# GpSimd waits for each indirect store, and for each tile's gathers, before it issues the next

## The reference

```python
x = layernorm(x + attention(x))            # 16 heads of 16, causal
x = layernorm(x + shared(x) + routed(x))
# routed: sigmoid scores over 16 experts, top 2 of (score + bias), the two scores scaled to sum 1;
# routed = sum over a token's two experts e of
#          weight_e * (silu(x @ gate_e) * (x @ up_e)) @ down_e      256 -> 2 x 128 -> 256
```

## Time and profile before

| | |
|---|---|
| Timed runs | 985.47, 985.3, 978.0 us |
| Span of the profiled execution | 975.7 us |
| Between its span and the median of the runs | 9.6 us |
| PE, DVE, ACT, POOL busy | 88%, 68%, 49%, 31% |
| Mean granted TensorE clock | 0.943 |
| Section 0's stores on GpSimd, first start to last start | 691.54 to 732.16 us |
| Pairs on PE | 737.83 to about 910 us |
| Section 1's gathers, first start to last start | 917.02 to 960.67 us |

### The profile page before, as it was taken

The page is one execution under the profiler, slowest core; times in us unless marked ns, Lnnn a source line. Parts: engine busy times, 40 slices in busy tenths (PEclk is TensorE's granted clock), DMA queues, the critical chain, the costliest instruction groups (busy, mean ns, idle before and its releaser), DMA issues. The chain is left out here.

```text
span 975.7 us, 18404 instructions
## 1 busy us (share of the span) xinstructions
PE 854.0 (88%) x5476; PEld 478.9 (49%) x5477; DVE 660.1 (68%) x1527; ACT 476.2 (49%) x686; POOL 300.0 (31%) x368
## 2 busy tenths in 40 slices
PE   7979799999999989999999997799898999999300
PEld 4635434444444434444444432687556777777200
DVE  6428688888888887888888870489892122466364
ACT  3423266656666656656666566455322444444100
POOL 3423312211112111221112211442477500464373
PEclk9979899999999999999999999889899999999755
DMA  8773855444764266425754000710126745766443
GB/s 285 193 205 131 162 67 75 100 97 59 131 85 89 36 117 118 68 38 106 130 66 57 9 2 25 235 65 23 60 103 210 232 137 152 207 207 211 157 126 95
DMA packets 82464, 113.95 MB, mean 117 GB/s; under 512 B 8945, under 2 KB 60401, under 8 KB 82417
## 3 DMA queue, kind: packets, MB, share of 16 engines
q1 hardware_dynamic: 57808, 78.01, 38.1%
q0 software_dynamic: 6720, 18.88, 5.9%
q10 hardware_dynamic: 17888, 16.41, 5.2%
HBM read 62.55 MB, written 50.33 MB: 116 GB/s over the span
## 5 line engine op out<-in xcount | busy, mean ns | idle before, releaser
L658 ACT ACTIVATE work<-ps 128x1024 f32<-128x1024 f32 (+3 forms) x384 | 293.8, 811 | 185.5 <-PE ps L725 185.3
L335 DVE TENSOR_REDUCE m_neg<-ps 128x1 f32<-128x512 f32 (+3 forms) x432 | 265.6, 662 | 29.2 <-PE ps L320 18.7
L629 POOL TENSOR_SCALAR_AFFINE_SELECT work<-work 128x512 f32<-128x512 f32 x128 | 81.2, 634 | 394.4 <-ACT work L658 390.0
L317 PE MATMUL ps<-stacks 96*128 96x512 bf16 (+3 forms) x528 | 151.9, 332 | 1.5 <-DVE m_neg L335 1.5
L725 PE MATMUL ps<-stacks 99*128 99x512 bf16 (+3 forms) x528 | 124.6, 329 | 6.4 <-PEq L371 4.8
L335 DVE TENSOR_REDUCE m_neg_late<-ps 128x1 f32<-128x384 f32 (+3 forms) x176 | 106.7, 636 | 27.4 <-PE ps L320 27.4
L740 PE MATMUL ps<-work,vg 128*32 128x512 f32 (+3 forms) x1056 | 112.5, 498 | 1.6 <-POOL work L629 1.6
L320 PE MATMUL ps<-mask_b,ident_b 128*128 128x128 bf16 x512 | 100.3, 223 | 0.0
L317 PEld LDWEIGHTS ps<-stacks 96*128 96x128 bf16 x528 | 50.0, 98 | 95.0 <-DVE m_neg L335 48.8
L1243 DVE TENSOR_TENSOR work<-work,ps 128x256 f32<-128x256 f32 x48 | 20.2, 421 | 106.7 <-ACT work L1062 106.7
L1421 PE MATMUL ps<-wgu,work 128*128 x384 | 91.7, 382 | 0.3 <-issue 0.3
(11 more groups left out here) (143 smaller groups left out, 1098.4 us busy)
## 6 DMA issues: line engine op xcount, KB each, us to landing
stacks<-qk_parts SPq DMA_DIRECT2D x132, 128.0 KB, 6.3
qk_parts<-work SPq DMA_DIRECT2D x32, 384.0 KB, 3.0
y_sorted<-work SPq DMA_DIRECT2D x8, 1536.0 KB, 9.9
work<-y_sorted SPq DMA_DIRECT2D x48, 256.0 KB
z_sorted<-work ACTq DMA_DIRECT2D x48, 256.0 KB
wgu<-qk_parts SPq DMA_DIRECT2D x60, 128.0 KB, 6.5
work<-in_xT SPq DMA_DIRECT2D x8, 512.0 KB, 4.8
work<-in_x SPq DMA_DIRECT2D x8, 512.0 KB, 3.6
```

Source lines behind the costliest of these rows:

```text
L317: mm = pe.matmul(dst, qs[r][0:KS, h0 + m, qt * P:(qt + 1) * P], ks[r][0:KS, h0 + m, half * CH:half * CH + w], start=True, stop=not diag)
L335: dve.tensor_reduce(dst, ps[:, bank, 0:heads * w].rearrange("p (h k) -> p h k", h=heads), AX.X, ALU.max, negate=True).then_inc(reduced, 1)
L629: pool.affine_select(out=blk_, in_=blk_, compare_op=ALU.is_ge, fill=0.0, base=0, pattern=[[0, GH], [1, P]], channel_multiplier=-1).then_in ...
L658: act.activation(probs[:, s + 2 * pair:s + 2 * pair + 2, off:CH], ps[:, SCORE_BANK + 2 * pair:SCORE_BANK + 2 * pair + 2, off:CH], ACT.Exp, ...
```

## The change

A constant `IN_FLIGHT = 1` is added. Before its j-th indirect store of a tile GpSimd now waits until all earlier stores of the section have landed. Before the first gather of a tile it waits until both gathers of the tile before have landed. The number and size of the DMAs, their order on GpSimd and everything on the other engines stay.

```diff
+IN_FLIGHT = 1
...
                 def scatter(t):
                     g = t // SEC_TILES
                     for j in range(TOPK):
+                        wait_count(pool, scattered[g], 16 * ((t - g * SEC_TILES) * TOPK + j + 1 - IN_FLIGHT))
                         pool.indirect_dma_start(
...
                 def gather(u):
                     wait_count(pool, both_added, u - ZSLOTS + 1)
+                    if u > 0:
+                        pool.wait_ge(gathered[(u - 1) % ZSLOTS], 16 * TOPK * ((u - 1) // ZSLOTS + 1))
                     for j in range(TOPK):
                         pool.indirect_dma_start(
```

## The result

The changed kernel takes 1096.03 us (median of 4 runs, 1093.02 to 1100.68); the kernel before, on the same chips, 981.65 us (974.74 to 985.47, 4 runs). The ratio is 1.117, with a 95% interval of 1.111 to 1.124; between the medians lie 114 us. The forecast was +113.5 us. Two of the runs further down, gathers0_early_store and act_deviation, hold one execution each that took 2174 and 1493 us; their ratios leave it out.

A forecast was written before the change was run, and what follows sets the result against it. The prediction took GpSimd's serial indirect stores and gathers, not busy PE, as bounding the changed stretches. Added to 985.3 us, 47 + 24 + 16 + 24.5 + 2 = 113.5 us gave 1099 us, range 1057 to 1142.

The forecast's parts named there:

- A: Section 0's stores: nothing covers them, 31 steps grow from 1.31 to 2.82 us, +47 us.
- R2: Rival: GpSimd wakes slowly, 0.8 us with issues of 1.23, in all stores and gathers; 1155 us, chance 0.10.
- R4: Rival: a store's landing is mostly queueing behind its own kind, so waits are free; 981 us, chance 0.01.
- B: Section 1's stores, behind section 0's pairs: steps of 3.52 us leave PE waiting at pair 24, +24 us.
- R1: Rival: loaded landings stay near 2.8 and 3.0 us, B and C nearly vanish; 1067 us, chance 0.20.
- C: Section 0's gathers, behind section 1's pairs: 5.0 us a tile against DVE's 3.55 us turn, +16 us.
- R3: Rival: stores and gathers under load land as late as 4.4 us each time; 1133 us, chance 0.08.
- D: Section 1's gathers, bare at the end: 15 steps of 4.49 us, 71.5 us instead of 47.0, +24.5 us.
- E: PE's clock: after the stall of B, PE restarts at the lower 1.2 GHz level, +2 us.
- the 9.6 us: Time from the profiled span of 975.7 us to the runs' median 985.3, taken as lying around the span, unchanged.

The follow-up runs named there:

- gathers0_early_store: Kernel before plus waits only in section 0's gathers, chunk 0's output store issued right behind tile 11's gathers; 1042.89 us, ratio 0.999.
- act_deviation: Kernel before without the waits, section 1's second-norm reciprocal deviations moved from GpSimd to DVE and ACT; 1040.52 us, ratio 0.995.
- gathers_one_wait: Kernel before plus waits only in the gathers, the both_added wait moved ahead of the previous tile's second gather; 1067.28 us, ratio 1.024.

## Why the prediction was right

**A** was right in its mechanism: bare, landing by landing. The wake of 0.31, taken from a store released by DVE, is 0.27 after a landing, and the issue stays at 0.96 where I took 1.07, the issue of a gather. 31 steps of 2.74 instead of 2.82 gave +44.4 instead of +47. R2 (wake 0.8) is out for a single wait, and R4 too: the landing alone is 2.40, what it was with others in flight.

**B** went as argued. Landings beside the loads have a median of 3.0, I took 3.1; the step there is 3.47 (797.11 to 870.00, 21 steps), I took 3.52. What I left out is that the first three or four stores of section 1 still go at the quiet step, before the loads run; the step over all 32 is 3.26. The gap is 19.7 us (22.2 by itself) for +24. R1 is answered in a way that I hadn't thought of: its condition, landings near 2.8 and 3.0, came nearly true, with medians of 3.0 and 3.1, and B and C did not vanish. By my own sum a landing of 3.0 is a step of 3.42 and a gap of 22 us, not the 10 that R1 was given. R3 falls: with landings of 4.4 every time the stores would have been 4.8 apart.

**C** was right in size, +18.9 for +16, but not in all of its parts. That output stores on GpSimd fall into its waiting "at no cost" was wrong: store(0) comes later with GpSimd, and DVE waits 10.1 us for it (2.2 before), of which about 4 count. The gathers land at a median of 3.1 where I had 3.3, and the second wait, from the sixth tile on, was not counted. The errors are of opposite sign.

**D** is the term that was mis-sized: +31.6 for +24.5. The step "0.31 + 1.38 + 2.8" misses that a gather has two waits, and that the one GpSimd blocks on then has an instruction of its own: 0.76 and 1.09 instead of 0.31 and 1.07. That is 0.47 a tile, 7 us over 15, and gathers_one_wait gives that back (67.9 instead of 75.7). R2's wake was true only where a gather has two waits, here and in C's later tiles.

**E** is small, as put: about 1.6 us in the two matmul groups behind the gap, for +2.

That the sum came out within 2 us of the 115 is luck. The terms were off by -2.6 (A), -5.7 (B with E), +2.9 (C) and +7.1 (D), and these nearly cancel. I also read the 9.6 us wrongly as lying around the span: the changed kernel's profiled execution took 1100.68 us at a span of 1098.8, 1.9 us more, so most of the 9.6 was probably the difference between one execution and another. It did no harm, since the sum uses the median alone.

What the forecast didn't ask is what unlimited stores cost. On the chips of the result no trace has a wait for "remote", and +115 is the price. On the third chip it is 49 us net (1092.64 against 1043.89), because the kernel before itself is some 60 us slower there; the changed kernel's own time is nearly the same on both (1096.03 and 1092.64).

What stays open: what the engines wait for in "remote". The Trainium skill, "Runtime: NRT & Kernel Launch", Instruction fetch mechanics, says that each sequencer fetches its instructions in blocks by a DMA queue of its own. If those queues had to wait for GpSimd's, it would fit a wait with no named releaser on ACT and DVE at once; no run here shows it. Why three of the chips used show it and others don't is open too.

## What to carry to other kernels

A row of these indirect DMAs issued without waiting costs the issue time of each (1.27 us here); a wait on each landing costs landing plus wake (2.67), and two in flight already get nearly all of it back (43.8 us for 32 stores, against 40.6 and 85.0). Ask of each such queue whether its end is on the path, and of each wait added whether it is the instruction's only one. And compare on more than one chip: where engines stand still without a named releaser beside a long train of indirect DMAs, keeping two stores in flight was worth 4%, and with gathers paced by their consumer and the deviations moved it was 5%.

## What was not expected of the hardware

- The second wait in front of an indirect DMA costs 0.5 us when GpSimd is blocked on a landing (idle 2.21 against 1.71), and nothing when both are passed (0.30).
- Indirect stores land in 2.40 us alone as well as with another behind them every 1.27 us.
- On three chips out of those used, the kernel before takes 1041 to 1045 us instead of 976 to 985, and the kernels traced there with unlimited stores have waits of ACT for an unnamed releaser, up to 30 us long, the longest of which end within 6 us of the start of a section's last store. Beside stores of which one is in flight there are none.
